# Early-fusion transformer block on one core: the 64-feature part of the attention scores as two one-pass products on stacked high and low parts

## The reference

```
xn   = layernorm(layernorm(h)) * ln_w                 # (8, 178, 192)
Q    = xn[:, None] * W_qk[None, :, None, :]           # head h scales the 192 features by W_qk[h]
attn = einsum('bhse,bhte->bhst', Q, Q) / sqrt(192)    # queries and keys are the same tensor
attn = softmax(where(causal, attn, -inf))
out  = einsum('bhst,bhte->bhse', attn, xn - mean(wte, axis=0)) / (position + 1)
h    = h + out.reshape(b, s, 12 * 192) @ W_o.T
```

## Time and profile before

| | us |
|---|---|
| median of three executions | 501.29 (500.12 to 502.48) |
| the profiled execution | 502.05 |
| its span, first to last instruction | 500.2 |
| PE busy in the span | 467.5 |
| DVE busy | 324.2 |
| ACT busy | 174.5 |
| POOL busy | 70.5 |

### The profile page before, as it was taken

The page is one execution under the profiler, slowest core; times in us unless marked ns, Lnnn a source line. Parts: engine busy times, 40 slices in busy tenths (PEclk is TensorE's granted clock), DMA queues, the critical chain, the costliest instruction groups (busy, mean ns, idle before and its releaser), DMA issues.

```text
span 500.2 us, 8643 instructions
## 1 busy us (share of the span) xinstructions
PE 467.5 (93%) x2672; PEld 400.7 (80%) x2672; DVE 324.2 (65%) x860; ACT 174.5 (35%) x566; POOL 70.5 (14%) x94
## 2 busy tenths in 40 slices
PE   5688999999999999999999998599999999999994
PEld 2365768967689766896668988599999999999994
DVE  6875787166861668527657847876666766667664
ACT  1364466045660455605420214122223222222221
POOL 6031111211112111000001422010000100001000
PEclk9798999999999999999979978899999999999997
DMA  8989999999999999650000000011111111111103
GB/s 207 250 267 208 212 209 203 205 212 211 212 213 212 213 213 213 137 95 1 1 0 1 1 21 1 9 36 42 32 29 37 36 40 32 29 37 36 24 1 89
DMA packets 30450, 52.86 MB, mean 106 GB/s; under 512 B 8342, under 2 KB 22479, under 8 KB 30045
## 3 DMA queue, kind: packets, MB, share of 16 engines
q0 software_dynamic: 7664, 39.98, 38.7%
q1 hardware_dynamic: 21548, 11.42, 9.1%
q10 hardware_dynamic: 1216, 1.21, 0.9%
HBM read 50.12 MB, written 1.09 MB: 102 GB/s over the span
## 4 chain that ended last, share of the span: by engine, by line
PE 85%; DVE 8%; issue 2%; ACT 2%; POOL 2%; DVEq 0%; POOLq 0%; ACTq 0%
PE bank L873 13%; PE bank L769 12%; PE bank L727 6%; PE bank L842 4%; PE bank L844 4%; PE bank L846 4%; PE bank L843 4%; PE bank L672 4%; PE bank L845 4%; PE bank L674 4%; PE bank L732 3%; PE bank L684 2%; PE bank L685 2%; PE bank L700 2%; PE bank L728 2%
## 5 line engine op out<-in xcount | busy, mean ns | idle before, releaser
L873 PE MATMUL bank<-wdn,hidT 128*128 128x192 f32 (+1 forms) x408 | 78.8, 330 | 5.9 <-DVE hidT L1101 5.9
L577 ACT ACTIVATE area_b<-bank,bcol 128x356 f32<-128x356 f32 x68 | 38.0, 558 | 132.2 <-PE bank L846 132.2
L1282 DVE SCALAR_TENSOR_TENSOR R<-bank,wts,R 128x192 f32<-128x192 f32 (+1 forms) x204 | 72.5, 411 | 8.1 <-issue 3.7
L495 ACT ACTIVATE pm<-bank,nmax 128x128 f32<-128x128 f32 x96 | 33.9, 365 | 112.0 <-DVE nmax L1010 112.0
L873 PEld LDWEIGHTS bank<-wdn,hidT 128*128 128x128 f32 (+1 forms) x408 | 67.5, 184 | 6.5 <-DVE hidT L1101 6.4
L1101 DVE SCALAR_TENSOR_TENSOR hidT<-bank,bcol,area_b 128x356 f32<-128x356 f32 x68 | 39.9, 587 | 49.0 <-PE bank L846 49.0
L769 PE MATMUL bank<-woT,oT 128*128 128x192 f32 (+1 forms) x432 | 71.6, 327 | 0.0
L769 PEld LDWEIGHTS bank<-woT,oT 128*128 128x128 f32 (+1 forms) x432 | 69.9, 182 | 0.5
L842 PE MATMUL bank<-xah,wah 128*128 128x356 f32 x136 | 54.4, 400 | 0.4 <-DVE lg L1059 0.4
L423 POOL DMA_DIRECT2D wacc<-in_L_attn_wte_dram x26 | 31.4, 1207 | 135.0 <-DMA wacc<-in_L_attn_wte_dram 135.0
L844 PE MATMUL bank<-xah,wal 128*128 128x356 f32 x136 | 45.2, 332 | 0.0
(11 more groups left out here) (183 smaller groups left out, 773.7 us busy)
## 6 DMA issues: line engine op xcount, KB each, us to landing
wacc<-in_L_attn_wte_dram POOLq DMA_DIRECT2D x28, 1344.0 KB, 12.6
woT<-in_L_attn_W_o_dram SPq DMA_DIRECT2D x1, 1728.0 KB, 16.7
oT<-in_x_dram SPq DMA_DIRECT2D x4, 384.0 KB, 9.4
wdn<-in_L_ffn_Wd_dram SPq DMA_DIRECT2D x16, 96.0 KB, 1.9
wacc<-wacc POOLq DMA_DIRECT2D x1, 1344.0 KB, 9.8
wra<-in_L_ffn_Wu_dram SPq DMA_DIRECT2D x16, 64.0 KB, 1.8
wrb<-in_L_ffn_Wu_dram SPq DMA_DIRECT2D x32, 32.0 KB, 2.1
wra<-in_L_ffn_Wg_dram SPq DMA_DIRECT2D x16, 64.0 KB, 1.9
```

The source lines that it names most:

```text
L577: act.activation(sil[:, sl, :], bank[sl][:, 0:CW], ACT.Silu, bias=bcol[:, (n // PAIRS) % 2, 0:1]).then_inc(silu_ready, 1)
L873: last = pe.matmul(o, hidT[:, sl, at:at + rows], wdn[:, k, :], start=True, stop=True)
L1282: last = dve.scalar_tensor_tensor(out=old, in0=src, scalar=wts[0:rows_, 3 * i + t, bass.ds(e, 1)], in1=old, op0=ALU.mult, op1=ALU.add)
```

## The change

The 64-feature operands become float32r (F32R, rounded) and use all 128 partitions. `xbu` holds the high (rounded) part of `xb` on both halves of the partitions, `xbv` the low part (`xb` minus the high part) on both halves. `qb` holds the high part of the scaled keys on partitions 0 to 63 and the low part on 64 to 127. The product with `xbu` gives high times (high + low), the one with `xbv` low times (high + low). Each float32 product on `xb` becomes two one-pass products on `xbu` and `xbv`. ACT writes two more copies per sample and `qb`'s high part as before; DVE makes the low parts: two operations per sample (`split_low`) and one per head (`query_lows`), 64x192 each. The two fills with zero go.

```diff
-        xb = sb("xb", [P, 2, SP])
+        xb = sb("xb", [64, 2, SP])
+        xbu = sb("xbu", [P, 2, SP], F32R)
+        xbv = sb("xbv", [P, 2, SP], F32R)
-        qb = part_of(area_b, 0, P, 2, 3, NH, 64)
+        qb = part_of(round_b, 0, P, 2, 3, NH, 64)
-            pool.memset(qb[64:P], 0.0).then_inc(s_pad, 1)
-            pool.wait_ge(s_pad, 3)
 # ACT, turn_out
                 act.activation(xa[:, b, :], bank[7][:, 0:SP], ACT.Copy).then_inc(xnT_ready, 1)
+                act.activation(xbu[0:64, b, :], bank[7][0:64, SP:2 * SP], ACT.Copy)
+                act.activation(xbu[64:P, b, :], bank[7][0:64, SP:2 * SP], ACT.Copy)
                 act.activation(xb[0:64, b, :], bank[7][0:64, SP:2 * SP], ACT.Copy).then_inc(xnT_ready, 1)
 # ACT, queries_b
-                    last.then_inc(qb_ready, 1)
+                    last.then_inc(qb_high, 1)
 # ACT, pair
+                    if u == 3 and not last:
+                        act.wait_ge(xnT_ready, 4 * i + 6)
+                        queries_b(0, 2 * i + 2, [0])
                     if u == 4 and not last:
-                        act.wait_ge(xnT_ready, 4 * i + 6)
-                        queries_b(0, 2 * i + 2, [0, 1])
+                        queries_b(0, 2 * i + 2, [1])
 # PE, scores
-                pe.matmul(split, xb[:, b, 0:P], qb[:, b, 0:2, h:h + GRP, :].rearrange("p c j t -> p j c t"),
-                          start=False, stop=False)
+                for x_ in (xbu, xbv):
+                    pe.matmul(split, x_[:, b, 0:P], qb[:, b, 0:2, h:h + GRP, :].rearrange("p c j t -> p j c t"),
+                              start=False, stop=False)
...
-                    pe.matmul(o, pair_b, xb[:, b, 0:S], start=False, stop=(k == 1), skip_group_check=True)
+                    pe.matmul(o, pair_b, xbu[:, b, 0:S], start=False, stop=False, skip_group_check=True)
+                    pe.matmul(o, pair_b, xbv[:, b, 0:S], start=False, stop=(k == 1), skip_group_check=True)
 # PE, queries_in
+                if g == 0:
+                    pe.wait_ge(xb_low, bt + 1)
 # DVE, new
+            def split_low(b, bt):
+
+                dve.wait_ge(xnT_ready, 2 * bt + 2)
+                for at in (0, 64):
+                    last = dve.tensor_tensor(xbv[at:at + 64, b, :], xb[:, b, :], xbu[0:64, b, :].bitcast(F32),
+                                             ALU.subtract)
+                last.then_inc(xb_low, 1)
+
+            def query_lows(b, bt, groups):
+
+                dve.wait_ge(xnT_ready, 2 * bt + 2)
+                for g in groups:
+                    dve.wait_ge(qb_high, UPB * bt + g + 1)
+                    for h in range(GRP * g, GRP * g + GRP):
+                        last = dve.scalar_tensor_tensor(out=qb[64:P, b, :, h, :], in0=xb[0:64, b, :].rearrange(
+                            "p (c t) -> p c t", c=3), scalar=w2b[:, h:h + 1], in1=qb[0:64, b, :, h, :].bitcast(F32),
+                            op0=ALU.mult, op1=ALU.subtract)
+                    last.then_inc(qb_ready, 1)
 # DVE, ahead of the loop
-            queries(0, 0)
+            split_low(0, 0)
+            queries(0, 0, [0])
+            query_lows(0, 0, [0])
+            queries(0, 0, [1, 2])
             keep(0, 0)
             keep(1, 0)
+            split_low(1, 1)
+            query_lows(0, 0, [1])
...
             embeds_out(3)
+            query_lows(0, 0, [2])
             queries(1, 1)
+            query_lows(1, 1, range(UPB))
 # DVE, pair
                         if u == 3:
                             keep(0, i + 1)
+                            split_low(0, 2 * i + 2)
                             queries(0, 2 * i + 2, [0])
                         if u == 4:
+                            query_lows(0, 2 * i + 2, [0])
                             queries(0, 2 * i + 2, [1, 2])
...
                 mix_out(5, U + 5)
                 if not last:
+                    query_lows(0, 2 * i + 2, [1])
                     keep(1, i + 1)
+                    split_low(1, 2 * i + 3)
+                    query_lows(0, 2 * i + 2, [2])
                     queries(1, 2 * i + 3)
+                    query_lows(1, 2 * i + 3, range(UPB))
```

More of the change, by code:

```diff
@@ L103, in early_fusion_kernel @@
         area_a = sb("area_a", [P, 2 * NH * SP])
-        area_b = sb("area_b", [P, 2 * NH * SP])
+        with nc.sbuf_tensor("area_b", [P, 2 * NH * SP], F32) as area_b:
+            pass
+        round_b = sb("round_b", [P, 2 * NH * SP], F32R)
         def part_of(area, at, *shape):
@@ L217, in early_fusion_kernel @@
         qa_ready = sem("qa_ready")
+        qb_high = sem("qb_high")
         qb_ready = sem("qb_ready")
+        xb_low = sem("xb_low")
         scores_main = sem("scores_main")
@@ L776, in _ @@
             turn_in(1, 1, 0)
-            pe.wait_ge(s_pad, 3)
+            pe.wait_ge(s_pad, 1)
             queries_in(0, 0)
@@ L944, in _ @@
             own.mark(dve.memset(mv[:], 1.0))
-            dve.memset(xb[64:P], 0.0).then_inc(s_pad, 1)
             dve.memset(pT1[:], 0.0).then_inc(s_pad, 1)
```

## The result

The changed kernel took 509.03 us (median of four; 506.16 to 512.54), the kernel before 501.81 beside it: ratio 1.0152, 95% interval 1.008 to 1.0224. Run again later, beside other kernels, it took 510.18 us (507.09 to 511.85), ratio 1.014 (1.009 to 1.0191). The forecast was 502.6, "the same", range 498.5 to 507.0. The sign was that of rivals 3, 4 and 5.

The account below looks back on a forecast made before the run. PE's matmuls were taken to bound most of the attention (busy 93%, 85% of the chain). A start loss of 7.8 us less pair gains of 0.85, 2 x 1.54 and 2.59 gave +1.3: 502.6 us, range 498.5 to 507.0.

Parts of the forecast that it names:

- rival 3: PE's stand ahead of mix(4) in three pairs lowers the clock: 1.5 to 5 us, middle 505.8; chance 0.2.
- 4: Rival: weight loads cost more, 178-column products at 0.16 us, saving 0.33 us a unit, 506.1 us; chance 0.12.
- 5: Rival: the products are not one-pass in this form, two records each, no saving, 509 us; chance 0.01.
- the three ends: Units 4, 5 to the next pair's 0: PE waits for DVE's divides, net gain only 0.45 us a pair.
- Its likeliest case: The prediction's own forecast, 502.6 us, with chance 0.46; its own spread reaches 504.
- The start: DVE's added work delays the first divide from 36.24 to 44.0 us: 7.8 us lost, bounds 6.5 and 9.3.
- The clock behind the start: Lower clock after PE's longer stand, from 47.7 us on: an even exchange plus 0.3 us, bounds -1.5 and +1.7.
- S: PE's saving per unit from one-pass products replacing float32 ones: 0.55 us, bounds 0.33 to 0.70.
- unit 1 of the second and third pair: Scores just behind the projection: only the main half of the saving counts, 0.39 us.
- the lows in the projection: 20 lows and a split_low, 7.2 us of DVE work behind mix_out(5), covered by idle; uncovered, 7 us a pair.
- 1: Rival: DVE's work is hidden everywhere and PE's saving of 13 us comes whole, 488 us; chance 0.06.
- 2: Rival: short steps, one-pass products scale with columns (0.08 us) and lows run at 0.27, 498.9 us; chance 0.15.

Follow-up runs that it names:

- the filling: Changed kernel plus eight unread bf16 matmuls into bank 7 ahead of mix(4) in the first three pairs: 506.01 us, ratio 1.0086 to the kernel before.
- the reordering: Changed kernel with keep, split_low and four queries behind unit 5's maxima, eight queries moved into the projection: 503.53 us, ratio 1.002 to the kernel before.
- PE's half alone: Changed kernel without DVE's low parts, zeros in their place; one-pass products and ACT's extra copies kept: 493.37 us, ratio 0.9821 to the kernel before.
- DVE's half alone: Kernel before with its float32 products, plus ACT's copies and all DVE low parts, multiplied by zeros: 516.41 us, ratio 1.0293.
- the new start: Changed kernel, DVE loop written out, sample 1's twelve lows after the first divide, ACT's third high-part group before unit 0's exponentials: 501.79 us, ratio 1.0001.
- both orders: Changed kernel with both moves, at the start and at the pair's end: 496.91 us, ratio 0.9889 to the kernel before.

## Why the prediction was wrong

**The step that failed is "The clock falls in the new gaps", put among the rivals with a chance of 0.2.** The gap itself was forecast (1.7 us, measured 1.98), and so was the end without a fall (PE 0.55 us ahead at the scores of unit 5, and the transposes 0.1 later, at 136.4: some 0.7 us more per end, measured 0.8). The fall was taken for unlikely because 0.8 us of standing caused none, and the sum has nothing for it. It came in two of three pairs of one profile and three of three of the other, at 1.3 to 2.9 us each: 3.7 and 4.4 us in the three ends. That it was PE's standing is shown by the filling (all ends at 13.03, no fall) and by the reordering (gap 0.72, no fall). "The granted clock has new falls between 60 and 210 us" was one of the prediction's own signs of being wrong. Its likeliest case could have had it: where PE stood 0.82 us and, behind its transposes, another 1.60, the lower clock followed.

On the stretches of the table under the result, the forecast and the first profile compare thus:

```
                                      forecast  measured
start, to the scores of unit 2           +7.8      +9.6
first pair, scores 2 to 5                -0.95      0.0
the three ends                           +1.95     +6.1
unit 0 to unit 1, with the projection    -1.65     -0.9
scores 1 to 5, second and third pair     -3.3      -2.7
scores 1 to 5, last pair                 -2.05     -2.0
everything after                         -0.55     +0.4
sum                                      +1.3     +10.5
```

The falls are the largest difference, about 4.4 of 9.2 us (3.7 in the ends, 0.7 behind the first). Without them the forecast would still have been too low, mostly at the start and in the clock behind it; this is also why rival 3, which did have the falls at 1.5 to 5 us, came to only 505.8. The median execution lost 7.2 us, not 10.5; which of these terms are smaller in it isn't known.

**The start was right in mechanism and too small: 7.8 forecast, 9.0 measured** (first copy of `xa` to first divide, 16.7 to 25.7 us). The steps behind ACT's copies into `xbu` are 0.33 us, not 0.23 (0.2); a `split_low` takes 0.75, not 0.6 (0.3). ACT's third group of high parts was there 1.6 us after its exponentials (34.74, and DVE waits for it until 36.34), not 1.4. The remaining 0.5 are small excesses of the other steps. The second `embeds_out` (34.95) waited for PE, but DVE would have stood for ACT's group in any case. The lows at 0.33 were exact: (4.03 - 0.40)/11.

**The clock behind the start: 0.3 forecast (bounds -1.5 and +1.7), about 1.2 measured.** The lower clock lasted from 41.5 to 55.1 us; before, it lasted from 40.4 to 43.8. Scores 2 to 5 of the first pair took 23.07 us, and 21.89 with PE's half alone, where the lower clock lasted as long as before.

**PE's saving per unit was right, what becomes of it was too large.** S is 0.54. But unit 1 of the second and third pair gives 0 to 0.1, not 0.39 (in the last pair 0.34). In the kernel before, the maxima of that unit already stand right behind the divide:

```profile
162.34 0.52 DVE L1024 TENSOR_TENSOR pt<-pt,rsum 128x356 f32<-128x356 f32 x1
162.89 0.69 DVE L1010 TENSOR_REDUCE nmax<-bank 128x4 f32<-128x512 f32 x1
```

PE's half alone has the same step there (4.57 us) as the kernel before and the changed one, without any work added to DVE. A shorter main product can't help where DVE is what comes last; I had read the nearly simultaneous end of the product as the cause. That is 0.3 to 0.4 us in each of two pairs. Unit 3 gave 0.2 to 0.3 (forecast 0.15), units 2 and 4 their 0.44 to 0.55.

**Right:** the lows in the projection cost nothing (the projection's stretch is shorter by S in every pair not disturbed, 22.99 against 23.54), and the first two residuals were late without anyone waiting, as forecast. The last pair gained 2.0 up to the scores of unit 5 (forecast 2.6 with the last S). The zero fills gave nothing back. The wte loads came later without anyone waiting.

**The rivals.** 1 and 5 fall with the ends and with S. 2 and 4 fall with the steps 0.24 and 0.11. The scale of the earlier trace rows would have given 0.08. The Trainium skill (TensorE: Matmul & The Clock Gate, LDWEIGHTS (loading the stationary operand)) has a weight load take its columns over 1.2 GHz, 107 ns for 128. The step of 0.11 agrees with it, though no run here varies the columns of a weight load. The 77 ns that the Trainium skill's formula (TensorE: Matmul & The Clock Gate, Back-to-back issue gap) gives for 178 columns by an estimate are not reached.

In sum, by medians measured side by side: one-pass products -8.9, low parts +14.2, both at once 2.6 more, together +7.9 us. By the profiles the 2.6 are the falls of the clock (3.7 and 4.4 us), less 1.4 by which the ends without a fall are shorter than the halves add up to.

## What to carry to other kernels

Work moved from the busiest engine to a half-idle one is free only where that engine idles in the order of the program: look at each place where the busiest engine already waits (the start, the hand-over between stages), since every instruction added ahead of such a place is paid in full. Shortening matmuls around a wait lengthens the wait, and a longer wait can also lower PE's clock for what follows; a few matmuls into a free bank tell in one run whether that is the loss. Here the order, not the amount, was at fault: the same operations in other places, with one loop written out for it, turned +1.5% into -1.1%.

## What the runs showed of the hardware that was not expected

- Behind 0.9 us of transposes and 1.98 us of standing, TensorE went to 1.2 GHz in seven of nine passes (two profiles of the changed kernel, one of that with the new start), at the latest 1.5 us into mix(4). Behind 1.43 to 1.46 us (DVE's half alone) it did in none of three, behind 1.22 (PE's half alone) in none of three, behind 0.72 to 0.77 in none of nine (the kernel before, the new order of the pair's end, both orders).
- Matmuls whose product nobody reads made a kernel faster: 5.2 us of them (24 of 0.22) took 4.35 us off the three ends, and the median was 4.2 us lower.
- A higher clock at the start was no gain at the end: 0.76 to 1.00 in 30 to 60 us left the median where it was or higher (506.05 and 507.73).
- The last 251 to 254 us, all but the same instructions in every kernel, had two lengths with the amount of lower clock in them: 251.4 to 251.9 us with 17.1 us of it up to 340 us, 252.9 to 253.5 with 20.5 to 23.9. A difference of 1.5 us between two single profiles can be this alone.
- The steps behind ACT's copies of 64x192 from PSUM to `xbu` are 0.32 to 0.34 us, that behind the 128x192 copy to `xa` 0.23. Whether the number format or the partitions make the difference, no run shows.
